# Two mixture-of-experts FFNs around an attention: idle turns on TensorE, ScalarE's relu ahead of its square, row statistics joined and a rounding cut in four on GpSimd

## The chip, the core and the metric

The kernel runs on one core of one Trainium2 chip. The metric is the device time of one execution in microseconds (us), as the median of several runs. The core has five engines that run side by side, each in its own order, and meet at semaphores: TensorE (PE, matrix products), VectorE (DVE), ScalarE (ACT), GpSimd (POOL) and SyncE (SP, which here only starts transfers). TensorE reads its operands from SBUF and writes into eight banks of PSUM. GpSimd works in SBUF only.

## The reference, cut to what matters

4096 tokens of width 128 pass three layers, each behind a layer norm without weights and each added to its input:

```python
x = x + 0.5 * ffn(_layernorm(x), ...)
x = x + attention(_layernorm(x), ...)       # 4096 memory keys and values, one head, plus bias bo
x = x + 0.5 * ffn(_layernorm(x), ...)       # the same weights again

# ffn: 8 experts, the best 2 of each token, hidden width 176, and a shared expert of the same width
scores = sigmoid(x @ gate_w.T);  _, sel = top_k(scores + expert_bias, 2)
h      = square(relu((x * score) @ w_up[e].T in bf16));  routed = h @ w_down[e].T
shared = square(relu(x @ shared_w_up.T)) @ shared_w_down.T      # fp32
out    = sum over the 2 experts + shared
```

## The kernel before

**Tiling.** The tokens lie as 32 tiles of 128 and are worked on in 8 groups of 512. In an FFN all eight experts are computed for each group: the hidden units of the experts fill 11 chunks of 128 rows, taken as six slots k = 0 to 5 (five pairs and a single chunk). For each slot TensorE makes `up(G, k)` (line 1130), VectorE takes relu times the routing weight (`relu_weighted`, line 904, line 901 for the single chunk), ScalarE squares (`square`, line 566), and TensorE adds `down(G, k)` (line 1139). The shared expert goes beside it in fp32: `shared_up_product` (1095), `shared_relu` on ScalarE (555), `shared_square` (560), `shared_down` (1146). `copy_yT` (576) takes the group's sum out of PSUM, `transpose_back` (1112) turns it, and `residual` (912) adds it to X.

**Ahead of the group.** Groups are prepared three ahead (`AHEAD`): row statistics on VectorE (`bn_stats`, 778, then four `bn_aggr`, 786, with a memset between), mean and inverse deviation on GpSimd (`inverse_deviation`, 389 to 392), `normalize` on GpSimd (399), transposes on TensorE (1072), `copy_xT` on ScalarE (543), a cast on GpSimd (`cast_xT`, 423), the gate product (1087), and the routing on VectorE (`route_group`, 16 small steps, lines 853 to 891) for two groups at a time: steps 0 to 8 in a group with even number, steps 9 to 15 in the next. `spread_weights` (GpSimd, 413), `transpose_weights` (1104) and `copy_wbc` (571) bring the weights to the hidden rows.

**Beside it.** In the first FFN GpSimd also splits the attention's keys and values into two fp32r parts, one block of 1024 columns in each group: `kv_hi` (a cast, 454) and `kv_lo` (a subtraction, 456). In the attention it makes `p_lo` (464).

**Order.** Everything is written out by hand: each engine runs its instructions in the order of the code, and a wait holds up all that stands behind it on that engine. G counts the groups of both FFNs (0 to 15), i those of one FFN, n the layer norms (0 to 7 first FFN, 8 to 15 attention, 16 to 23 second FFN). Names are buffers that several things share: `probsT` also holds the hidden rows, `E` the routing weights and the staged keys, `probs` and `xq` the transposed input, `banks` is all of PSUM.

## Time and profile before

| | us |
|---|---|
| median of 3 runs (lowest, highest) | 672.46 (672.07, 672.78) |
| the profiled execution, its own time | 673.28 |
| its span in the trace | 671.6 |
| busy in it: TensorE, VectorE, ScalarE, GpSimd | 614.0, 535.2, 461.3, 381.2 |

The first FFN takes the span up to about 119 us, the attention goes on to about 581 us, the second FFN to the end. Busy times are sums over stages with different limits, so the shares don't tell what a change in one stage is worth. For that the chain of waits is read: it follows the last instruction back, at each step to what released it. The timeline of one engine then shows what stands beside such a step. Where a line says `x2`, two instructions are merged.

### The profile page before, as it was taken

What the parts mean: (1) busy time and instruction counts of PE and PEld (TensorE: products, weight loads), DVE (VectorE), ACT (ScalarE), POOL (GpSimd) and SP (SyncE); (2) the same over time, 40 slices, a digit from 0 to 9 for tenths busy, and PEclk for the clock granted to TensorE, in tenths of its full rate; (3) what the DMA queues carried; (4) which work ended last, traced back from release to release, by engine and by line L of the source; (5) the groups of instructions that cost most, each with busy time, mean ns of one, the idle gap of its engine ahead of it and who ended that gap; (6) DMA issues with size and microseconds to landing.
All of it is one profiled execution on the core that took longest, in us unless ns stands there. A gap on an engine that the chain in (4) does not pass through costs nothing.

```text
span 671.6 us, 9169 instructions
## 1 busy us (share of the span) xinstructions
PE 614.0 (91%) x2784; PEld 431.5 (64%) x2800; DVE 535.2 (80%) x968; ACT 461.3 (69%) x765; POOL 381.2 (57%) x378
## 2 busy tenths in 40 slices
PE   3888989769889999999999999999999997999997
PEld 2445434547667877777777778787777866645542
DVE  4799877748888888887797897887898764799885
ACT  3576778436668767777677786776776863577886
POOL 3856660025367766767687587586687874533100
PEclk9899999869999999999999999999999996999999
DMA  8011110042563553743734626527446330000000
GB/s 296 2 53 42 61 34 0 4 122 62 127 151 86 142 129 77 167 103 89 167 91 120 154 65 158 122 69 176 103 97 153 86 77 1 0 18 16 32 33 31
DMA packets 35555, 59.06 MB, mean 88 GB/s; under 512 B 8539, under 2 KB 9139, under 8 KB 35379
## 3 DMA queue, kind: packets, MB, share of 16 engines
q1 hardware_dynamic: 31891, 53.75, 31.8%
q10 hardware_dynamic: 3616, 4.73, 2.7%
q8 instruction: 23, 0.38, 0.3%
q14 instruction: 25, 0.20, 0.1%
HBM read 8.12 MB, written 2.10 MB: 15 GB/s over the span
## 4 chain that ended last, share of the span: by engine, by line
PE 64%; DVE 19%; issue 6%; ACT 4%; POOL 2%; SPq 2%; ACTq 1%; DMA 1%; DVEq 0%; POOLq 0%
PE banks L1254 7%; PE banks L1256 7%; PE banks L1255 7%; PE banks L1295 7%; PE banks L1297 6%; PE banks L1296 6%; PE banks L1274 4%; DVE bank_max L1007 4%; PE banks L1130 4%; DVE E L1002 3%; PE banks L1139 3%; DVE probsT L904 3%; PE banks L1146 3%; PE banks L1305 2%; PE banks L1095 2%
## 5 line engine op out<-in xcount | busy, mean ns | idle before, releaser
L464 POOL TENSOR_TENSOR p_lo<-probsT,p_hi 128x768 fp32r<-128x768 f32 (+1 forms) x128 | 226.4, 1773 | 173.5 <-ACT p_hi L659 173.2
L1007 DVE TENSOR_REDUCE bank_max<-banks 128x1 f32<-128x1024 f32 x128 | 156.1, 1219 | 34.3 <-PE banks L1256 33.5
L659 ACT ACTIVATE p_hi<-probsT 128x768 fp32r<-128x768 f32 (+1 forms) x128 | 104.5, 816 | 23.0 <-PE banks L1297 19.1
L1254 PE MATMUL banks<-kv_lo,q_parts 128*128 128x512 f32 x256 | 112.9, 441 | 5.1 <-ACT E L677 3.6
L566 ACT ACTIVATE probsT<-probsT 128x1024 bf16<-128x1024 bf16 x96 | 92.2, 980 | 34.5 <-DVE probsT L904 31.3
L1002 DVE STREAM_TRANSPOSE E<-E 128x1024 f32<-128x1024 f32 x92 | 113.5, 1234 | 0.4 <-ACT E L677 0.2
L904 DVE SCALAR_TENSOR_TENSOR probsT<-banks,E 128x1024 bf16<-128x1024 f32 x80 | 95.5, 1218 | 22.0 <-PE banks L1130 20.2
L1295 PE MATMUL banks<-p_hi,kv_lo 128*128 128x512 f32 x256 | 108.7, 424 | 0.4 <-ACT attended L696 0.3
L651 ACT ACTIVATE p_hi<-banks 128x256 fp32r<-128x256 f32 (+1 forms) x128 | 52.3, 408 | 81.2 <-PE banks L1274 81.0
L677 ACT ACTIVATE E<-banks,neg_max 128x1024 f32<-128x1024 f32 x92 | 102.3, 1112 | 6.7 <-DVE neg_max L1013 4.8
L1296 PE MATMUL banks<-p_lo,kv_hi 128*128 128x512 f32 x256 | 102.9, 402 | 0.0
L1297 PE MATMUL banks<-p_hi,kv_hi 128*128 128x512 f32 x256 | 102.7, 401 | 0.0
L1256 PE MATMUL banks<-kv_hi,q_parts 128*128 128x512 f32 x256 | 102.6, 401 | 0.0
L1255 PE MATMUL banks<-kv_hi,q_parts 128*128 128x512 f32 x256 | 102.4, 400 | 0.0
L995 DVE TENSOR_TENSOR p_lo<-banks,p_hi 128x256 fp32r<-128x256 f32 (+1 forms) x128 | 56.1, 438 | 45.5 <-ACT p_hi L651 45.1
L1274 PE MATMUL banks<-ident,probs 128*128 128x128 f32 x272 | 53.9, 282 | 10.9 <-ACT probs L687 6.7
L1274 PEld LDWEIGHTS banks<-ident,probs 128*128 128x128 f32 x272 | 37.2, 144 | 33.7 <-DVE p_lo L995 7.4
L1254 PEld LDWEIGHTS banks<-kv_lo,q_parts 128*128 128x128 f32 x256 | 49.2, 192 | 14.0 <-ACT E L677 4.7
L1295 PEld LDWEIGHTS banks<-p_hi,kv_lo 128*128 128x128 f32 x256 | 48.7, 190 | 13.6 <-issue 2.7
L1130 PE MATMUL banks<-E,wup_b 128*128 128x512 bf16 x166 | 50.3, 384 | 7.0 <-ACT probsT L555 6.1
L1297 PEld LDWEIGHTS banks<-p_hi,kv_hi 128*128 128x128 f32 x256 | 48.6, 190 | 12.4
L1256 PEld LDWEIGHTS banks<-kv_hi,q_parts 128*128 128x128 f32 x256 | 48.8, 191 | 11.6
(110 smaller groups left out, 887.5 us busy)
## 6 DMA issues: line engine op xcount, KB each, us to landing
probsT<-E SPq DMA_DIRECT2D x248, 128.0 KB, 2.4
probsT<-E SPq DMA_DIRECT2D x168, 64.0 KB, 2.0
E<-in_keys_values SPq DMA_DIRECT2D x8, 512.0 KB, 3.5
probsT<-E ACTq DMA_DIRECT2D x56, 64.0 KB, 2.4
out<-X SPq DMA_DIRECT2D x8, 256.0 KB, 2.1
X<-in_x SPq DMA_DIRECT2D x1, 1280.0 KB, 9.1
probsT<-E ACTq DMA_DIRECT2D x8, 128.0 KB, 4.1
X<-in_x SPq DMA_DIRECT2D x3, 256.0 KB, 5.3
```

The source lines that it names most:

```text
L464: pool.tensor_tensor(moved_part(p_lo, ring), moved_pair(ring // UP, ring % UP), moved_part(p_hi, ring).bitcast(fp32), ALU.subtract).then_i ...
L659: act.activation(moved_part(p_hi, ring), moved_pair(ring // UP, ring % UP), ACT.Copy).then_inc(moved_hi_done, 1)
L904: dve.scalar_tensor_tensor(hidden[:, k, :, :], up_banks[PAIR_BANK[k]], 0.0, spread.unsqueeze(1).to_broadcast([P, 2, N]), ALU.max, ALU.mult ...
L1002: dve.transpose(half, half).then_inc(squares_done, 1)
L1007: dve.tensor_reduce(bank_max[:, i % 2, h:h + 1], score_pair(u, i, h).rearrange("p b n -> p (b n)"), AX.X, ALU.max).then_inc(bank_max_done, 1)
L1254: pe.matmul(bank, qh, kl, start=True, stop=False)
L1255: pe.matmul(bank, ql, kh, start=False, stop=False)
L1256: pe.matmul(bank, qh, kh, start=False, stop=True).then_inc(scores_done, 1)
L1274: last = pe.transpose(TB[:, at_column:at_column + P], own_exponentials(w, t)[:, c * P:(c + 1) * P], ident[:, :])
L1295: pe.matmul(OB, vl, hi, start=(c == 0), stop=False)
L1296: pe.matmul(OB, vh, lo, start=False, stop=False)
L1297: pe.matmul(OB, vh, hi, start=False, stop=(c == KC - 1)).then_inc(pv_done, 1)
```

## The change

Five things, all around the FFNs:

- GpSimd takes over, for the layer norms n = 4 to 8, what `bn_aggr` did: `join_halves` makes mean and variance of a row from the two halves that `bn_stats` leaves. Eight small instructions stand where three were, and VectorE's memset and four `bn_aggr` go. VectorE's next `bn_stats` waits for GpSimd's reads instead.
- The subtraction that makes `kv_lo` is cut into four quarters of 256 columns, issued one behind the other without a wait between them.
- On ScalarE `square(G, 0)` goes behind `shared_relu(G)` and `copy_yT(G - 1)`, in all groups but the very first.
- TensorE turns the identity 24 times before its first real work: 12 when the constants are set, 8 when the first statistics are there, 4 when the first inverse deviation is there.
- The first group of X is loaded in two halves, by SP's and by ScalarE's queue.

```diff
+def joins_on_pool(n):
+    return AHEAD < n <= ATTENTION_LN
...
-            sp.dma_start(X[:, 0:GT, :], x[:, 0:GT, :]).then_inc(x_loaded[0], 16)
+            sp.dma_start(X[:, 0:GT // 2, :], x[:, 0:GT // 2, :]).then_inc(x_loaded[0], 16)
...
+            def join_halves(n):
+
+                step = POOL_STEPS * (n - AHEAD - 1)
+                means = stats[:, :, :].rearrange("p t (a b) -> p t a b", b=3)[:, :, :, 1]
+                sums = stats[:, :, :].rearrange("p t (a b) -> p t a b", b=3)[:, :, :, 2]
+                pool.tensor_scalar(half_means[:, :, :], means, -0.5, None, ALU.mult).then_inc(joined, 1)
+                pool.tensor_tensor(squares_sum[:, :], sums[:, :, 0], sums[:, :, 1], ALU.add).then_inc(joined, 1)
+                pool.wait_ge(joined, step + 1)
+                pool.tensor_tensor(half_gap[:, :], half_means[:, :, 0], half_means[:, :, 1], ALU.subtract
+                                   ).then_inc(joined, 1)
+                pool.tensor_tensor(neg_mean[:, :], half_means[:, :, 0], half_means[:, :, 1], ALU.add
+                                   ).then_inc(moments_read, 1)
+                pool.wait_ge(joined, step + 3)
+                pool.tensor_tensor(gap_squared[:, :], half_gap[:, :], half_gap[:, :], ALU.mult).then_inc(joined, 1)
+                pool.tensor_scalar(squares_sum[:, :], squares_sum[:, :], 1.0 / D, EPS, ALU.mult, ALU.add
+                                   ).then_inc(joined, 1)
+                pool.wait_ge(joined, step + 5)
+                pool.tensor_tensor(var_eps[:, :], gap_squared[:, :], squares_sum[:, :], ALU.add
+                                   ).then_inc(moments_read, 1)
+                pool.wait_ge(moments_read, 2 * n + 2)
+                pool.tensor_tensor(rstd[:, :], var_eps[:, :], minus_half[:, :], ALU.pow).then_inc(rstd_done, 1)
...
-                        pool.tensor_tensor(kv_lo[:, i, :], kv_stage[:, i % 2, :], kv_hi[:, i, :].bitcast(fp32),
-                                           ALU.subtract).then_inc(kv_lo_done, 1)
+                        for a in range(0, KVW, KVW // 4):
+                            part = slice(a, a + KVW // 4)
+                            last = pool.tensor_tensor(kv_lo[:, i, part], kv_stage[:, i % 2, part],
+                                                      kv_hi[:, i, part].bitcast(fp32), ALU.subtract)
+                        last.then_inc(kv_lo_done, 1)
...
+            act.dma_start(X[:, GT // 2:GT, :], x[:, GT // 2:GT, :]).then_inc(x_loaded[0], 16)
...
-                    square(G, 0)
                     if f or i:
                         shared_relu(G)
+                    if i:
+                        copy_yT(G - 1)
+                    square(G, 0)
                     if f and i == 0:
                         copy_y(LAST)
-                    if i:
-                        copy_yT(G - 1)
...
             def aggregate(n):
+                if joins_on_pool(n):
+                    return
...
+            def warm_up():
+
+                pe.wait_ge(consts_set, 1)
+                turn_identity(12)
+                pe.wait_ge(stats_done, 1)
+                turn_identity(8)
+                pe.wait_ge(rstd_done, 1)
+                turn_identity(4)
```

ScalarE, around the start of group 2 in the first FFN, before. Line 566 is `square`, 555 the shared relu, 576 `copy_yT`, 543 `copy_xT`:

```order
24 L566 ACTIVATE probsT<-probsT 128x512
25 L566 ACTIVATE probsT<-probsT 128x1024
26 L555 ACTIVATE probsT<-banks 88x1024
27 L576 ACTIVATE probsT<-banks 128x512
28 L543 ACTIVATE xq<-banks 128x512
29 L566 ACTIVATE probsT<-probsT 128x1024
```

The same place after, where `square` is line 615, the relu 604, `copy_yT` 625 and `copy_xT` 592:

```order
25 L615 ACTIVATE probsT<-probsT 128x512
26 L604 ACTIVATE probsT<-banks 88x1024
27 L625 ACTIVATE probsT<-banks 128x512
28 L615 ACTIVATE probsT<-probsT 128x1024
29 L592 ACTIVATE xq<-banks 128x512
30 L615 ACTIVATE probsT<-probsT 128x1024
```

The square of the group's slot 0 has moved behind the relu and `copy_yT`; it now stands directly ahead of `copy_xT`.

GpSimd, from one group to the next in the first FFN, before. Line 454 is `kv_hi`, 456 `kv_lo`, 389 to 392 the inverse deviation, 413 the spread weights, 423 the cast of the next input:

```order
38 L454 CAST kv_hi<-E 128x1024
39 L456 TENSOR_TENSOR kv_lo<-E,kv_hi 128x1024
40 L389 TENSOR_TENSOR neg_mean<-moments,minus_one 128x4
41 L390 TENSOR_TENSOR var_eps<-moments,eps 128x4
42 L392 TENSOR_TENSOR rstd<-var_eps,minus_half 128x4
43 L413 COPY probsT<-weight 128x1024
44 L423 CAST E<-xq 128x512
```

The same place after:

```order
43 L499 CAST kv_hi<-E 128x1024
44 L503 TENSOR_TENSOR kv_lo<-E,kv_hi 128x256 x4
45 L408 TENSOR_SCALAR half_means<-stats 128x8
46 L409 TENSOR_TENSOR squares_sum<-stats 128x4
47 L411 TENSOR_TENSOR half_gap<-half_means 128x4
48 L413 TENSOR_TENSOR neg_mean<-half_means 128x4
49 L416 TENSOR_TENSOR gap_squared<-half_gap 128x4
50 L417 TENSOR_SCALAR squares_sum<-squares_sum 128x4
51 L420 TENSOR_TENSOR var_eps<-gap_squared,squares_sum 128x4
52 L423 TENSOR_TENSOR rstd<-var_eps,minus_half 128x4
53 L458 COPY probsT<-weight 128x1024
54 L468 CAST E<-xq 128x512
```

One subtraction has become four, and the three instructions ahead of the spread weights have become eight.

## Rows read from the trace of the kernel before

**Rows 1.** The page's first part: busy us, share of the span, instructions.

```profile
PE 614.0 (91%) x2784; PEld 431.5 (64%) x2800; DVE 535.2 (80%) x968; ACT 461.3 (69%) x765; POOL 381.2 (57%) x378
```

**Rows 2.** Chain of waits, groups 2 to 4 of FFN one: start, duration, what.

```profile
55.78 1.86 DVE route L877
...
62.91 1.01 ACT probsT L555
...
66.78 0.44 PE banks L1104 x4
...
76.01 0.79 PE banks L1087 x8
76.80 0.46 PE banks L1130 x2
```

**Rows 3.** Timeline of VectorE, group 4: start, duration, line, operation.

```profile
78.43 0.35 DVE L872 TENSOR_SCALAR route<-expz 128x64 f32<-128x64 f32 x1
...
79.40 1.85 DVE L877 TENSOR_TENSOR route<-route,ebias 128x64 f32<-128x64 f32 x1
```

**Rows 4.** Timeline of GpSimd in the same stretch.

```profile
77.69 1.04 POOL L454 CAST kv_hi<-E 128x1024 fp32r<-128x1024 f32 x1
78.81 2.36 POOL L456 TENSOR_TENSOR kv_lo<-E,kv_hi 128x1024 fp32r<-128x1024 f32 x1
```

**Rows 5.** Line 877, whole span: duration ns lowest/median/highest, first and last start.

```profile
L877 DVE TENSOR_TENSOR route<-route,ebias x9: 192/224/1855, 13.3 to 634.3; 128x64 f32<-128x64 f32 x7, 128x32 f32<-128x32 f32 x2
```

**Rows 6.** Timeline of VectorE in FFN two, where GpSimd is idle.

```profile
633.46 0.18 DVE L872 TENSOR_SCALAR route<-expz 128x64 f32<-128x64 f32 x1
```

**Rows 7.** Timeline of both engines at 575 us: VectorE waits beside two GpSimd instructions.

```profile
575.62 1.28 POOL L464 TENSOR_TENSOR p_lo<-probsT,p_hi 128x512 fp32r<-128x512 f32 x1 [0.80 <-ACT p_hi L659]
576.88 1.91 POOL L399 TENSOR_SCALAR xn<-X,neg_mean,rstd 128x128 f32<-128x128 f32 x4
...
575.88 1.30 DVE L817 CAST E<-probs 128x512 bf16<-128x512 f32 x1
```

**Rows 8.** Timeline of ScalarE, start of group 3, then of group 4.

```profile
61.95 1.06 ACT L566 ACTIVATE probsT<-probsT 128x1024 bf16<-128x1024 bf16 x1 [0.50 <-DVE probsT L904]
...
72.34 1.06 ACT L566 ACTIVATE probsT<-probsT 128x1024 bf16<-128x1024 bf16 x1 [0.48 <-DVE probsT L904]
73.31 1.00 ACT L555 ACTIVATE probsT<-banks 88x1024 f32<-88x1024 f32 x1
...
74.75 0.60 ACT L543 ACTIVATE probs<-banks 128x512 f32<-128x512 f32 x1
```

**Rows 9.** Timeline of GpSimd, group 4, then the spread weights of group 3.

```profile
73.74 0.20 POOL L390 TENSOR_TENSOR var_eps<-moments,eps 128x4 f32<-128x4 f32 x1
74.02 1.01 POOL L392 TENSOR_TENSOR rstd<-var_eps,minus_half 128x4 f32<-128x4 f32 x1
...
64.83 1.04 POOL L413 COPY probsT<-weight 128x1024 f32<-128x1024 f32 x1 [0.20 <-DVE weight L891]
```

**Rows 10.** Timeline of VectorE, statistics of group 4.

```profile
72.23 0.86 DVE L778 BATCH_NORM_STATS2 stats<-X 128x6 f32<-128x128 f32 x4
...
73.23 0.28 DVE L786 BATCH_NORM_AGGREGATE moments<-stats 128x2 f32<-128x6 f32 x3
```

**Rows 11.** Chain of waits, group 5 of the second FFN.

```profile
639.77 1.01 ACT probsT L555
```

**Rows 12.** Timeline of TensorE, first group, then a later shared up product.

```profile
8.43 1.09 PE L1072 MATMUL banks<-ident,xn 128*128 128x128 f32 x4 [8.43 <-DVE xn L797]
...
18.52 3.62 PE L1095 MATMUL banks<-xq,sup_s 128*88 128x512 f32 x4
...
47.70 1.88 PE L1095 MATMUL banks<-probs,sup_s 128*88 128x512 f32 x4
```

**Rows 13.** Chain of waits, first microseconds.

```profile
0.72 3.49 DMA X<-in_x
```

**Rows 14.** TensorE by stretch: length, busy us (instructions), granted clock, transfers' share, GB/s.

```profile
25.00:26.00 1.00, 0.24 (x2) 0.77 0.00 0
```

More of the change, by code:

```diff
@@ L59, with moments_before @@
 Q_HALF = 5
+def joins_on_pool(n):
+    return AHEAD < n <= ATTENTION_LN
+POOL_STEPS = 5
+def moments_before(n):
+    return sum(not joins_on_pool(k) for k in range(n))
 ATTENTION_LN = GROUPS
@@ L772, in statistics @@
             def statistics(n, g):
-                wait(dve, moments_done, n)
+                if joins_on_pool(n - 1):
+                    dve.wait_ge(moments_read, 2 * n)
+                else:
+                    wait(dve, moments_done, moments_before(n))
                 if n >= SECOND_LN:
@@ L781, in aggregate @@
             def aggregate(n):
+                if joins_on_pool(n):
+                    return
                 dve.wait_ge(stats_done, n + 1)
@@ L1141, in down, with turn_identity @@
                 last.then_inc(down_done, 1)
+            def warm_up():
[5 more added lines that the diff above has]
+                turn_identity(4)
+            def turn_identity(times):
+                for _ in range(times):
+                    pe.transpose(up_banks[0][:, 0, 0:P], ident[:, :], ident[:, :])
             def shared_down(G):
```

14 lines of the change are left out of this document (11 added, 3 removed).

## The prediction, made before the changed kernel ran

> **What bounds the kernel now.** I read the page's busy times first, to see that no engine is full: TensorE is busy 614.0 of 671.6 us, the others less [rows 1]. So waits decide, and they differ by stage. The change touches only the FFNs, so I then followed the chain of waits through two neighbouring groups of the first FFN [rows 2]. It has two kinds of stretch. From 66.78 us to 76.80 us every link is TensorE: the odd group is bound by its products. Ahead of that, from the relu of slot 3 in group 2, the chain leaves TensorE: routing steps and relus on VectorE, then the shared relu on ScalarE (62.91 us), then TensorE again. The longest link there is line 877, 1.86 us for an addition on 128x64 values. The same instruction has a median of 0.22 us over its nine times [rows 5]. In group 4 it ends at 81.25 us, just behind GpSimd's `kv_lo`, which ends at 81.17 us [rows 3, 4]: it waits for the SBUF port that GpSimd holds. This happens in groups 0, 2 and 4, where `kv_lo` stands beside it, with 1.6 us of waiting in each: some 4.8 us of the span.
>
> **The quarters.** A GpSimd subtraction takes 1.28 us at 512 columns [rows 7] and 2.36 us at 1024 [rows 4], so 2.1 ns a column and 0.2 us besides; at 256 columns I estimate 0.7 us, and 2.8 us for the four, 0.45 us more for each block. GpSimd is busy for 57% of the span [rows 1] and, with the block done, stands idle until the next statistics, so that is hidden. Line 877 starts 0.6 us behind `kv_lo` and would find the port free after 0.1 us, if the waiting engine gets it between two instructions. Rows 7 say it does: a cast of VectorE waits for one GpSimd instruction, ends at 577.18 us, and the next four on GpSimd take 1.91 us instead of 1.76. But line 877 isn't the only step with two SBUF inputs. Line 855 behind it now meets the second quarter (about 0.4 us), and lines 858 and 862 behind slot 4's relu the third and fourth (0.1 to 0.3 us). So of 1.6 us I count 1.0 us at slot 4's relu and 0.9 us at the next group's slot 0.
>
> The Trainium skill (page "SBUF — State Buffer", section "Who interferes with whom") says that the shared port pair is an exclusive lock held for a whole instruction, and that a VectorE instruction with two SBUF inputs contends with a GpSimd instruction that reads SBUF; lines 877 and 456 bear that out, 81.25 us against 81.17 us.
>
> **ScalarE's order.** At the start of an odd group the shared relu stands behind `square` of slot 0, and that waits 0.50 us for VectorE's slot 0 [rows 8]. With the relu first it can start behind the square of slot 5, at 61.45 us instead of 62.91 us, and `copy_yT` and `copy_xT` follow 0.5 us earlier than now. TensorE's next products then wait no more for the relu but for slot 0 and slot 1 from VectorE, so VectorE's time is what counts. At the start of an even group it goes the other way: there the relu waits for the shared product and starts at 73.31 us either way, and the square, which today runs in ScalarE's idle time at 72.34 us, is put between `copy_yT` and `copy_xT` [rows 8]. `copy_xT` (74.75 us) and with it the cast on GpSimd come 0.9 us later, `down` of slot 0 waits for the square until 75.8 us, and the gate product, now at 76.01 us, starts at about 76.3 us. **Cost 0.3 us** at the relu of slot 3, which opens the VectorE stretch.
>
> GpSimd's 0.9 us has a second effect: `kv_hi` moves to about where line 872 starts. Line 872 runs 0.35 us beside it today, 0.18 us where GpSimd is idle [rows 3, 6]. At worst it waits for all of `kv_hi` (0.9 us), at best it goes ahead of it. Walking through both orders, slot 4's relu comes 0.56 us or 0.96 us earlier than now, slot 0's 0.45 or 0.65 us. I take 0.55 us, all of the above included.
>
> **The join.** VectorE loses the memset and four `bn_aggr`. `bn_stats` ends at 73.09 us and the last `bn_aggr` at 73.51 us [rows 10]; since neighbours on VectorE overlap by some 0.07 us, that is 0.35 us, in groups 0 to 4. On GpSimd's way from the statistics to the inverse deviation a dependent instruction starts 0.28 us behind its source (73.74 us to 74.02 us) [rows 9]. Five such steps, counting those whose wait an independent one fills in part, and the power at 1.01 us make 2.4 us, against 1.94 us now (73.09 us to 75.03 us). So the inverse deviation comes 0.5 us later, measured from `bn_stats`. In even groups the cast behind it waits for `copy_xT` anyway. In odd groups the spread weights stand behind it; they start 0.20 us behind its end today [rows 9] and would be 0.34 us late. They are done at 65.87 us now and TensorE transposes them at 66.78 us [rows 2], so 0.8 us of that is spare, and a group that comes forward by d at slot 0 comes forward by d + 0.45 us at the weights' transposes, where VectorE's 0.35 us is already in. The new wait, `bn_stats` on GpSimd's reads, has a whole group of time.
>
> **By pair of groups.** Groups 2 and 3: 0.55 + 0.45 = **1.0 us**. Groups 4 and 5: group 5 has no statistics, so **0.6 us**. Groups 0 and 1: no change of ScalarE's order in group 0, but the join is there 1.0 us longer in GpSimd's order and shifts `kv_hi` onto line 872; slot 0 gains 0.3 to 0.9 us, the pair **0.9 us**. Groups 6 and 7 have neither routing nor gate; relu first and square first come out within 0.1 us, since slot 1's relu and square decide. First FFN: **2.5 us less**.
>
> **The second FFN** has only the new order on ScalarE. Group 0 there pays 0.45 us (`copy_y` and `copy_xT` stand behind the square), given back but for 0.3 us in group 1; the next pair costs 0.1 us, and groups 4 and 5 gain 0.2 us, since the relu is on the chain there [rows 11]. **0.2 us more.**
>
> **The start.** The first transposes take 1.09 us for four, and the shared product takes 3.62 us there and 1.88 us later [rows 12]. That is the lower clock of 1.2 GHz (the record of the granted clock starts later, so the durations tell it). The 24 turns at 0.27 us each (1.09 us / 4) fill 1.9 to 8.4 us, so the first real transposes at 8.43 us start neither later nor, I think, on the critical path if faster: GpSimd's second normalization doesn't wait for them, and the gaps up to 18.5 us stay. The shared product at 18.52 us is what the next group waits for, and I take it to be slow still. Its worth is 0 to 0.1 us. The load of X takes 3.49 us [rows 13]; half the bytes on each of two queues, with the next load close behind, I put at 0.1 us less (0.3 less to 0.2 more). **0.1 us less.**
>
> **Sum:** 0.9 + 1.0 + 0.6 - 0.2 + 0.1 = 2.4 us less. From the profiled execution, 673.28 us, that gives 670.9 us; the median of the runs before stands 0.8 us under it, so the predicted median is 672.46 - 2.4 = **670.1 us**.
>
> **Rivals.**
> 1. *The clock stays up.* If the turns keep TensorE at 2.4 GHz until 22 us, the shared product ends 1.7 us sooner, and the next group's input with it: 670.1 - 1.8 = 668.3 us. Against it: between the first transposes and 13 us TensorE has only the gate product. After it first rose, it fell back within the stretch from 25 to 26 us, whose mean is 0.77 of full speed, with TensorE busy for 0.24 us [rows 14]. Chance 0.1.
>
> The Trainium skill (page "TensorE: Matmul & The Clock Gate", Part 1) says that the throttled state is the default and activity releases it, which is what the turns would use; by that rule the time would be this rival's only if the activity afterwards holds it.
>
> 2. *More comes through.* Line 872 goes ahead of `kv_hi`, the later steps miss the quarters, and relu first shortens the odd groups by more than VectorE's share: 0.7 us more in each of three pairs, 668.0 us. Chance 0.15.
> 3. *Eaten.* `kv_hi` takes line 872's time in full, the join makes the weights late, and TensorE, the bound of odd groups, gives nothing back: 671.1 to 673 us, 672.0 us as the middle. Chance 0.2.
> 4. *Slower: the four quarters hold the port together.* They are issued without a wait between them. If VectorE doesn't get in, line 877 waits until the end of the fourth: `kv_lo` ends 0.45 us later than now and starts up to 0.9 us later, so each of three groups loses up to 1.3 us instead of gaining 0.55, and with 0.3 us of the new order the total is 3 x 0.9 us more: 675 us. It decides as soon as VectorE misses two boundaries. Rows 7 speak against it, though GpSimd's instructions there are of two kinds. Chance 0.1.
>
> **Numbers.** My forecast (669.1 to 671.1 us, 0.45) and the rivals above. A measurement of this kernel tells about 0.2% (1.3 us) from no change. Faster by more than that: 0.45 + 0.1 + 0.15 = 0.70; within: 0.20; slower: 0.10. The range leaves out the slower rival and the tail of the first two together: 667.4 to 672.9 us.
>
> **What would show it.** Line 877 in groups 0, 2 and 4 at 0.3 us or less, with line 872 up to 1.1 us in one or two of them; `kv_lo` in four of 0.7 us; `copy_xT` of even groups behind the square; the chain of odd groups without the shared relu; the shared product at 18.5 us still at 3.6 us (if at 1.9, rival 1). Line 877 at 2 us or more in spite of the quarters is rival 4. Wrong I would be if the attention's length changed by more than 1 us, since nothing in it is touched.

## The result and the profile after

| | median us | lowest to highest | runs |
| --- | --- | --- | --- |
| before | 672.36 | 670.02 to 673.72 | 15 |
| changed | 674.08 | 671.56 to 677.78 | 15 |

The ratio is 1.0038, with an interval of 1.0023 to 1.0053: the changed kernel is **slower by 0.4%**, where I had forecast 2.4 us less. The ratio is estimated from the runs together with its interval and isn't the quotient of the medians: these lie 1.7 us apart, and the ratio stands for 2.6 us. Below, what a part is worth in us is its ratio less one, times the median before. The profiled execution of the changed kernel took 676.66 us, near the upper end of its runs, with a span of 675.0 us. A second one (e8, below) took 674.34 us.

The page's first part for the changed kernel, which answers to [rows 1]:

```profile
PE 623.6 (92%) x2808; PEld 435.8 (65%) x2824; DVE 530.2 (79%) x943; ACT 460.4 (68%) x765; POOL 390.2 (58%) x427
```

VectorE has 25 instructions less, GpSimd 49 more and TensorE the 24 turns. TensorE is busy for 9.6 us more, although the turns take 6.0 us of it (two rows of 2.82 and 3.15 us). The other 3.6 us fit the stretches at the lower clock below; I haven't added them up.

The part of the change that I had worked out in most detail came out. The timeline of VectorE in group 4 of the first FFN (start, duration, line, operation), which answers to [rows 3]; lines 926, 931 and 909 are lines 872, 877 and 855 of before:

```profile
76.26 0.72 DVE L926 TENSOR_SCALAR route<-expz 128x64 f32<-128x64 f32 x1
...
77.59 0.22 DVE L931 TENSOR_TENSOR route<-route,ebias 128x64 f32<-128x64 f32 x1
...
78.11 0.39 DVE L909 TENSOR_TENSOR route<-route,best 128x64 f32<-128x64 f32 x1
```

The addition of 1.85 us takes 0.22 us. Line 926 takes 0.72 us instead of 0.35 us. GpSimd in the same stretch shows why, beside [rows 4] and [rows 9]: the first instruction of the join, its last (the power), and then `kv_hi` across the start of line 926, with `kv_lo` in four of 0.70 us behind it.

```profile
70.54 0.25 POOL L408 TENSOR_SCALAR half_means<-stats 128x8 f32<-128x8 f32 x1 [0.37 <-DVE stats L830]
...
72.06 1.04 POOL L423 TENSOR_TENSOR rstd<-var_eps,minus_half 128x4 f32<-128x4 f32 x1
...
75.88 1.04 POOL L499 CAST kv_hi<-E 128x1024 fp32r<-128x1024 f32 x1
77.01 2.78 POOL L503 TENSOR_TENSOR kv_lo<-E,kv_hi 128x256 fp32r<-128x256 f32 x4
```

The chain of waits through the same groups (start, duration, what) has no long piece of line 931 left, but two pieces that [rows 2] doesn't have: ScalarE's `copy_yT` and `square` ahead of TensorE at the start of group 4, and a gap of 2.37 us in group 5, behind which four transposes take 1.09 us, as at the lower clock in [rows 12].

```profile
71.51 0.58 ACT probsT L625
72.09 0.95 ACT probsT L615
...
73.09 0.61 PE banks L1193 x2
...
86.40 2.37 issue
88.77 1.09 PE banks L1158 x4
```

### The profile page after: what moved, and what is told of

The parts are those of the page before. It is cut to its first block, busy times and chain, and to the rows that moved or that the text cites. A ratio compares the mean times of both kernels' runs of the same rounds, so it can differ in the third digit from the quotient of the medians.

```text
span 675.0 us, 9236 instructions
## 1 busy us (share of the span) xinstructions
PE 623.6 (92%) x2808; PEld 435.8 (65%) x2824; DVE 530.2 (79%) x943; ACT 460.4 (68%) x765; POOL 390.2 (58%) x427
## 4 chain that ended last, share of the span: by engine, by line
PE 56%; DVE 18%; issue 6%; SPq 6%; ACT 5%; POOL 4%; DMA 3%; ACTq 1%; DVEq 0%; POOLq 0%
PE banks L1321 6%; SPq L330 6%; PE banks L1323 6%; PE banks L1322 6%; PE banks L1362 5%; PE banks L1363 5%; PE banks L1364 5%; DVE probsT L958 4%; PE banks L1341 4%; PE banks L1193 3%; DVE bank_max L1061 3%; PE banks L1184 3%; DVE E L1056 3%; PE banks L1213 3%; PE banks L1149 2%
## 5 line engine op out<-in xcount | busy, mean ns | idle before, releaser
L1363 PEld LDWEIGHTS banks<-p_lo,kv_hi 128*128 128x128 f32 x256 | 48.8, 191 | 11.7 <-issue 1.7
```

The lines of the kernel that those rows point to most:

```text
L1363: pe.matmul(OB, vh, lo, start=False, stop=False)
```

## How the traces are compared

All the kernels below have the same instructions on TensorE around the shared down product, which opens once in each group. So the distance from one start of that product to the next is a ruler. Its start in groups 1 and 2 of the kernel before, and of the kernel of e2:

```profile
44.69 1.88 PE L1146 MATMUL banks<-probsT,sdown_s 88*128 88x512 f32 x4
...
54.99 0.60 PE L1146 MATMUL banks<-probsT,sdown_s 88*128 88x512 f32 x1
```

```profile
46.02 1.88 PE L1146 MATMUL banks<-probsT,sdown_s 88*128 88x512 f32 x4
...
56.80 0.59 PE L1146 MATMUL banks<-probsT,sdown_s 88*128 88x512 f32 x1
```

54.99 - 44.69 = 10.30 us before, and 10.78 us in e2. From such rows comes this table, us, with the last column the distance between groups 0 and 7 of the second FFN (1 to 2 is from group 1 to group 2 of the first):

| kernel | ratio (interval) | 1 to 2 | 2 to 3 | 3 to 4 | 4 to 5 | 5 to 6 | 2nd FFN |
| --- | --- | --- | --- | --- | --- | --- | --- |
| before | | 10.30 | 13.31 | 10.31 | 14.87 | 9.47 | 74.49 |
| before again (e16) | | 10.30 | 13.32 | 10.30 | 14.89 | 9.47 | 74.49 |
| e1 quarters | 0.9952 (0.9934 to 0.9970) | 10.30 | 11.97 | 10.30 | 13.52 | 9.47 | 74.49 |
| e2 ScalarE's order | 1.0055 (1.0032 to 1.0078) | 10.78 | 13.64 | 10.78 | 15.19 | 9.83 | 75.43 |
| e3 join | 0.9993 (0.9971 to 1.0014) | 10.31 | 13.43 | 10.31 | 15.15 | 9.48 | 74.19 |
| e4 start | 1.0015 (0.9994 to 1.0037) | 10.30 | 13.31 | 10.30 | 14.87 | 9.48 | 74.48 |
| e5 all but the order | 0.9968 (0.9952 to 0.9984) | 10.30 | 12.10 | 10.30 | 13.82 | 9.47 | 74.20 |
| e6 quarters, join | 0.9945 (0.9926 to 0.9964) | 10.31 | 12.09 | 10.31 | 13.81 | 9.47 | 74.21 |
| e7 quarters, order in odd groups | 0.9961 (0.9936 to 0.9985) | 10.30 | 11.99 | 10.30 | 14.12 | 10.58 | 74.51 |
| e8 the change again | 1.0022 (1.0000 to 1.0044) | 10.77 | 12.06 | 10.77 | 14.74 | 10.67 | 75.14 |
| the change | 1.0038 (1.0023 to 1.0053) | 10.78 | 12.05 | 10.78 | 15.35 | 9.87 | 75.13 |
| e11 quarters, copies first | 0.9977 (0.9954 to 0.9999) | 11.25 | 12.29 | 11.24 | 13.86 | 9.82 | 74.49 |
| e12 e6, order in groups 1, 3 | 0.9961 (0.9939 to 0.9982) | 10.30 | 11.99 | 10.30 | 13.83 | 9.47 | 74.20 |
| e13 order in group 5 | 1.0011 (0.9995 to 1.0027) | 10.30 | 13.31 | 10.31 | 15.55 | 10.47 | 74.49 |
| e14 order in the second FFN | 1.0008 (0.9990 to 1.0027) | 10.31 | 13.31 | 10.30 | 14.87 | 9.47 | 75.43 |

Where the code of a stretch is the same and the clock stays up, the distances agree within 0.02 us, so a shift of 0.1 us in this table is a real one. The times of whole runs spread over 2.6 to 8.8 us for one kernel.

The last column opens at the shared down product of group 0 and leaves out what the order does inside that group. From the shared up product to the shared down product of group 0 in the second FFN, in the kernel before and in e14:

```profile
581.31 1.88 PE L1095 MATMUL banks<-xq,sup_s 128*88 128x512 f32 x4
...
588.64 1.88 PE L1146 MATMUL banks<-probsT,sdown_s 88*128 88x512 f32 x4
```

```profile
579.29 1.88 PE L1101 MATMUL banks<-xq,sup_s 128*88 128x512 f32 x4
...
587.07 1.88 PE L1152 MATMUL banks<-probsT,sdown_s 88*128 88x512 f32 x4
```

That is 7.33 us against 7.78 us. The other thirteen profiles with the square first there have 7.31 to 7.33 us, the other three with the relu first there (the change, e2, e8) 7.77 or 7.78 us: 0.45 us more, on top of the last column.

## The parts alone: e1 to e4

**e1**, `kv_lo` in quarters:

```
-    pool.tensor_tensor(kv_lo[:, i, :], kv_stage[:, i % 2, :], ...
+    for a in range(0, KVW, KVW // 4):
+        ...
```

> The kernel before with kv_lo in four quarters alone. The prediction's step: VectorE's addition of 128x64 values behind slot 3's relu falls from 1.86 us to 0.3 us or less in groups 0, 2 and 4, kv_lo takes 4 x 0.7 us; 0.5 to 1.0 us in each of three pairs of groups comes forward, so about 2 us less in the first FFN. Theory A (the attention's loss is the clock's, set off by an earlier start): the first FFN is 2 us shorter and the attention 1 to 3 us longer, ratio 0.998 to 1.002. Theory B (the attention's loss comes from the turns of the identity or the split load): nothing is lost behind, ratio 0.997.

668.23 us against 671.51 us, ratio 0.9952: 3.2 us less. In groups 2 and 4 the stretch is shorter by 1.34 and 1.35 us, where I had counted 1.0 us. The groups 0 and 1 can be read only roughly, since the clock differs at the start: the shared down product of group 1 starts at 42.45 us in e11, which has e1's code up to there, but at 44.89 us in e1 itself, and at 44.00 to 44.69 us in five profiles without the quarters (before, e10, e13, e14, e16). VectorE in group 4 (line 880 is line 877 of before, line 858 line 855):

```profile
77.28 0.35 DVE L875 TENSOR_SCALAR route<-expz 128x64 f32<-128x64 f32 x1
...
78.25 0.23 DVE L880 TENSOR_TENSOR route<-route,ebias 128x64 f32<-128x64 f32 x1
...
78.77 0.39 DVE L858 TENSOR_TENSOR route<-route,best 128x64 f32<-128x64 f32 x1
```

The addition gains 1.62 us, and the two later steps give 0.17 and 0.10 us back. Nothing eats the gain behind the FFN: theory B holds here, and the prediction's rival 4 falls.

**e2**, the shared relu ahead of the square of slot 0, in all groups:

```
-                    square(G, 0)
                     if f or i:
                         shared_relu(G)
+                    if i:
+                        copy_yT(G - 1)
+                    square(G, 0)
```

> The kernel before with ScalarE's shared relu ahead of the square of slot 0 alone. The prediction: about 0 in the first FFN (odd groups gain up to 0.5 us, even groups lose 0.3 us and push kv_hi onto VectorE), 0.2 us more in the second. The pair of profiles says 0.65 us more in the second FFN. If that is this order's: ratio 1.001, the attention's length as before. If the second FFN's loss was the clock's, its length here is within 0.2 us of the kernel before.

674.73 us, ratio 1.0055: 3.7 us **more** (interval 2.1 to 5.2), the largest effect of all parts. The traces place 3.4 us of it: 2.0 us in the first FFN between groups 1 and 7, and in the second 0.45 us in group 0 and 0.94 us behind it. ScalarE at the start of group 4, which answers to [rows 8]; then TensorE (`down` of slot 0) and VectorE's line 872:

```profile
75.38 1.02 ACT L555 ACTIVATE probsT<-banks 88x1024 f32<-88x1024 f32 x1 [1.38 <-PE banks L1095]
...
76.77 1.05 ACT L566 ACTIVATE probsT<-probsT 128x1024 bf16<-128x1024 bf16 x1
77.72 0.59 ACT L543 ACTIVATE probs<-banks 128x512 f32<-128x512 f32 x1
...
78.11 0.38 PE L1139 MATMUL banks<-probsT,wdown_b 128*128 128x512 bf16 x1 [0.38 <-ACT probsT L566]
...
81.05 0.69 DVE L872 TENSOR_SCALAR route<-expz 128x64 f32<-128x64 f32 x1
```

The relu starts when the shared product ends, in either order. Before, the square had been done in the time that ScalarE waited for it ([rows 8], 72.34 us). Now it comes behind, and TensorE waits for it. Laid on the kernel before by the relu's start, `down` of slot 0 is 0.4 us later; laid by the preceding shared down product the whole group is 0.48 us later. `copy_xT` is 0.83 us later, and with it the cast, the normalization and `kv_hi` on GpSimd, which so meets line 872: 0.69 us instead of 0.35 us. Each even group costs 0.48 + 0.34 = 0.82 us. The chain then runs over VectorE, so all that follows is late by as much.

**e3**, the join on GpSimd:

```
-                pool.wait_ge(moments_done, n + 1)
+                if joins_on_pool(n):
+                    ...
+                    join_halves(n)
+                    return
```

> The kernel before with the rows' statistics of groups 3 to 8 joined on GpSimd alone. The prediction: 0.35 us less on VectorE in each of groups 0 to 4, the inverse deviation 0.5 us later; 0.2 to 0.4 us a pair, about 0.8 us less in the first FFN, ratio 0.999. If the join makes the spread weights late, the first FFN is as long as before or longer by up to 0.5 us. Nothing behind the first FFN changes by theory B; by theory A the attention takes part or all of the gain back.

672.09 us beside 671.51 us, but ratio 0.9993: no difference that can be measured. The table says what it does: 0.12 us more from group 2 to 3, 0.28 us more from 4 to 5, and 0.30 us less from group 0 to 1 of the second FFN, where the join isn't. GpSimd's way from the statistics is the cause of the first two: in the changed kernel it takes 72.06 + 1.04 - 70.54 = 2.56 us from the start of its first instruction to the end of the power. In group 4 of the kernel before, the cast behind the power stood idle for 0.39 us for ScalarE's copy:

```profile
75.42 0.61 POOL L423 CAST E<-probs 128x512 bf16<-128x512 f32 x1 [0.39 <-ACT probs L543]
```

In e6 it starts right behind the power and waits for nothing, so the later power pushes it and `kv_hi` behind it, which comes 0.31 us later than in the same group of e1 (9.69 us and 9.38 us behind the shared down product of group 3). VectorE in group 4 of e6, which has both edits:

```profile
75.73 0.64 DVE L925 TENSOR_SCALAR route<-expz 128x64 f32<-128x64 f32 x1
```

That is 0.29 us more than in e1 (0.35 us). The gain of the second FFN I can't explain: VectorE's row for slot 5's relu there shows a wait of 0.20 us put down to no other engine in e1 and none in e6, in the same code. It isn't chance: the step from group 0 to 1 there is 12.57 or 12.58 us in all six profiles with the join and 12.86 or 12.87 us in the twelve without.

**e4**, the start: the turns and the load in halves:

```
-            sp.dma_start(X[:, 0:GT, :], x[:, 0:GT, :]).then_inc(x_loaded[0], 16)
+            sp.dma_start(X[:, 0:GT // 2, :], x[:, 0:GT // 2, :]).then_inc(x_loaded[0], 16)
...
+            act.dma_start(X[:, GT // 2:GT, :], x[:, GT // 2:GT, :]).then_inc(x_loaded[0], 16)
...
-                    pe.wait_ge(consts_set, 1)
+                    warm_up()
```

> The kernel before with the start's edits alone: TensorE's 24 turns of the identity, and the load of X in two halves on two queues. Theory B (the attention's loss comes from here, from the split load's queues or the turns): the attention is 2 to 4 us longer and the ratio is 1.003 to 1.006. Theory A: the load lands about 0.4 us later, the first FFN is 0 to 0.4 us longer, the rest as before, ratio 1.000 to 1.001.

672.16 us, ratio 1.0015 with 1 inside its interval, and the attention takes 475.9 us beside 476.2 us before: it is not the start's edits that lengthen it. Theory B, which I held for that part, is wrong. The sum of the four parts is -0.48% - 0.07% + 0.55% + 0.15% = +0.15%, and 1.0038 and 1.0022 were measured for the whole.

## Together: e5, e6 and e8

**e5** is the changed kernel without the order:

```
+                    square(G, 0)
                     if f or i:
                         shared_relu(G)
-                    if i:
-                        copy_yT(G - 1)
-                    square(G, 0)
```

> The changed kernel with ScalarE's old order (square of slot 0 ahead of the shared relu), all else of the change kept. If the order is what makes the changed kernel slower, as the part alone says (ratio 1.0055, 3.7 us): 1.0038 - 0.0055 = 0.998, so 670 us beside a kernel before of 671.5 us, and the first FFN is some 2 us shorter and the second some 0.6 to 1.0 us shorter than in the changed kernel. If the parts disturb each other in the attention instead: the ratio stays above 1.001 and the attention is 2 us or more longer than before.

669.38 us, ratio 0.9968. With the order it is 672.97 us on the same chip (e8): the order costs 3.6 us inside the change as alone. **It is what made the change slower**: without it the change would have been faster by 0.3%. The table says where, e8 less e5: 0.47 us in each of the steps 1 to 2 and 3 to 4 and nothing from 2 to 3 (there the join has already brought `kv_hi` onto line 872, so the order has nothing to add), 0.92 us from 4 to 5, 1.20 us from 5 to 6, and 0.94 us in the second FFN, 4.0 us, and with the 0.45 us of the second FFN's group 0 it is 4.4 us in all.

**e6** keeps only `kv_lo` in quarters and the join (diffs of e1 and e3).

> The kernel before with the two edits that gained alone: kv_lo in quarters and the join on GpSimd. Sum of the parts: 0.9952 and 0.9993, so 0.9945 (667.8 us). If the join stands in the quarters' way on GpSimd, or TensorE bounds what is left, 0.9955 or more.

667.79 us, ratio 0.9945, as the sum of its parts: faster than both kernels, and the lowest ratio of all. e1 alone is within its interval, so what the join adds to it isn't shown.

**e8** is the changed kernel again, with no edit.

> The changed kernel once more, for a second profile. If the 4 us that its first profile loses in the attention between 200 and 210 us belong to the change, they are there again. If it is the clock's chance in one execution, the attention is within 1.5 us of the kernel before, the time is again 1.002 to 1.005, and the loss stands in the two FFNs.

Ratio 1.0022, attention 476.1 us beside 480.3 us in the first profile. The 4 us that the first profile loses between 200 and 210 us aren't the change's. There ScalarE's exponentials wait for SP's moves of strips, and TensorE idles behind them. The first profile of the change, ScalarE; then TensorE by stretch in it, and in the kernel before again (e16): length, busy us (instructions) of PE, PEld, DVE, ACT, POOL, granted clock, transfers' share, GB/s.

```profile
202.46 1.11 ACT L726 ACTIVATE E<-banks,neg_max 128x1024 f32<-128x1024 f32 x1 [3.25 <-DMA probsT<-E]
```

```profile
200.00:205.00 5.00, 2.71 (x13) 1.94 (x12) 2.36 (x3) 2.54 (x5) 1.37 (x2) 0.95 0.65 137
205.00:210.00 5.00, 5.00 (x18) 3.94 (x17) 3.21 (x5) 2.91 (x7) 4.39 (x3) 0.71 0.28 66
```

```profile
200.00:205.00 5.00, 4.05 (x11) 3.22 (x12) 2.74 (x3) 3.73 (x7) 3.03 (x2) 0.66 0.38 94
```

The kernel before has the same wait (2.80 us) and a fall of the clock in its second profile, e16, and neither in its first; the changed kernel's second profile (e8) has a wait of 2.23 us. Over the eighteen profiles of this study the attention, whose code is the same but for the first rows' statistics, takes 471.1 to 480.3 us from the last shared down product of the first FFN to the first of the second.

## Which groups, and which step: e7, e11, e12, e13, e14

**e7**, quarters, and the relu first in the odd groups of the first FFN only:

```
+                    relu_first = f == 0 and i % 2 == 1
+                    if not relu_first:
+                        square(G, 0)
...
+                    if relu_first:
+                        square(G, 0)
```

> kv_lo in quarters and the relu first in the odd groups of the first FFN only (groups 1, 3, 5, 7); the even groups and the second FFN keep the square first. The prediction's step: odd groups gain up to 0.5 us each, so 0.5 to 1.0 us less than quarters alone, ratio 0.9945. The trace of the order alone says that the odd groups lose 0.3 us each, since slot 1's square comes 0.2 us later and stands on the chain: 0.6 us more than quarters alone, ratio 0.996.

Both expectations miss. Groups 1 and 3 are as long as in e1 within 0.02 us: the odd group neither gains nor loses. In e2, laid over the kernel before at the shared down product of group 1, the relu of group 3 starts 0.74 us earlier, while VectorE's steps are 0.82 us late ahead of the relu and 0.82 us late behind it. The clearer view is e7 beside e1. ScalarE's relu and VectorE's slot 1 in group 3, first e1, then e7:

```profile
61.77 1.00 ACT L558 ACTIVATE probsT<-banks 88x1024 f32<-88x1024 f32 x1
...
63.54 1.22 DVE L907 SCALAR_TENSOR_TENSOR probsT<-banks,E 128x1024 bf16<-128x1024 f32 x1
```

```profile
57.78 1.00 ACT L558 ACTIVATE probsT<-banks 88x1024 f32<-88x1024 f32 x1
...
61.11 1.22 DVE L911 SCALAR_TENSOR_TENSOR probsT<-banks,E 128x1024 bf16<-128x1024 f32 x1
```

Measured from the shared down product of group 1 (44.89 us and 42.44 us), the relu comes at 15.34 us instead of 16.88 us, 1.54 us earlier, and VectorE's step at 18.67 us instead of 18.65 us. The relu and VectorE had been equally late; taking one away leaves the other. Group 5 costs 0.60 + 1.11 = 1.7 us, by another mechanism (e13).

**e11**, quarters, and in the even groups of the first FFN the order relu, `copy_yT`, `copy_xT`, square:

```
+                    even = f == 0 and i and i % 2 == 0
+                    if not even:
+                        square(G, 0)
...
                         copy_xT(n + AHEAD, G + AHEAD, i + AHEAD, xT_bank)
...
+                    if even:
+                        square(G, 0)
```

> kv_lo in quarters, and in the even groups of the first FFN the order relu, copy_yT, copy_xT, square of slot 0: the copy that GpSimd's cast waits for goes ahead of the square, which in the change it stands behind. Two causes are told apart. Group 1 to 2 (shared down to shared down): 10.30 us with the square first, 10.78 us in the change; if the late square on TensorE's path is the cause, it is 10.9 us or more here; if the late copy_xT is, 10.3 us. Group 2 to 3: 11.97 us with quarters alone, and 0.35 us more in the change, put down to kv_hi that comes onto VectorE's line 872 because copy_xT is late; with copy_xT early that part is gone and line 872 takes 0.35 us or less, not 0.70 us. Ratio 0.996 to 0.998, against 0.9952 of quarters alone.

The first cause is decided: 11.25 us, 0.95 us more, so it is the late square that TensorE waits for. The second expectation misses: `kv_hi` is on time and line 872's counterpart takes 0.22 us, yet group 2 to 3 is 0.32 us longer than in e1. TensorE and VectorE in group 2 (line 879 is line 872 of before, line 884 line 877):

```profile
50.73 0.38 PE L1146 MATMUL banks<-probsT,wdown_b 128*128 128x512 bf16 x1 [0.99 <-ACT probsT L569]
```

```profile
53.52 0.22 DVE L879 TENSOR_SCALAR route<-expz 128x64 f32<-128x64 f32 x1
...
54.36 0.78 DVE L884 TENSOR_TENSOR route<-route,ebias 128x64 f32<-128x64 f32 x1
```

VectorE's steps are later against GpSimd, which isn't, so the addition now falls on a quarter of `kv_lo` (0.78 us instead of 0.23 us). A shift of one engine doesn't remove the meeting, it moves it to another step.

**e12**, e6 with the relu first in groups 1 and 3 (the diff of e7 with `i in (1, 3)`):

> kv_lo in quarters, the join, and the relu first in groups 1 and 3 alone. With both off its path (statistics' tail and relu) the odd group can come forward, where each alone gave nothing: 0.4 us less in group 3 and as much in group 1 than quarters and join (0.9945), and no late q_high in group 5: 0.9935. If the two together give nothing either: 0.9945, and group 2 to 3 is 12.09 us as there.

668.57 us, ratio 0.9961: not better than e6. Group 2 to 3 is 11.99 us, 0.10 us less than in e6 where 0.4 us had been expected. A third wait takes over, the spread weights from GpSimd, late by the join. In group 3 of e12 they end at 63.58 us, and TensorE, idle for 0.31 us, starts to transpose them:

```profile
62.54 1.04 POOL L458 COPY probsT<-weight 128x1024 f32<-128x1024 f32 x1
```

```profile
63.67 0.63 PE L1161 MATMUL banks<-ident,probsT 128*128 128x128 f32 x4 [0.31 <-issue]
```

**e13**, the kernel before with the relu first in group 5 alone (the diff of e7 with `i == 5`):

> The kernel before with the relu first in group 5 of the first FFN alone. There ScalarE's q_high stands behind slot 1's square; with the relu first TensorE reaches its wait for q_low 0.9 us earlier, so it idles 2.37 us instead of 1.49 us (as in e2, e7, e8), and the end of the wait stays. If that longer idle stretch lets the clock fall in a part of the runs (it did in e7, e8 and the changed kernel, not in e2; 1.1 to 1.7 us each): ratio 1.0010 to 1.0020. If the clock there is chance either way: 1.0000.

Ratio 1.0011, interval 0.9995 to 1.0027: in the middle between the two expectations, and open by the times. The trace shows the mechanism. TensorE in group 5, the project product, the gap, and what follows:

```profile
87.34 1.10 PE L1241 MATMUL banks<-xq,wq_scaled 128*128 128x512 f32 x2
88.28 0.59 PE L1136 MATMUL banks<-E,wup_b 128*128 128x512 bf16 x2
91.24 0.63 PE L1110 MATMUL banks<-ident,probsT 128*128 128x128 f32 x4 [2.37 <-issue]
...
92.19 1.49 PE L1136 MATMUL banks<-E,wup_b 128*128 128x512 bf16 x3
93.47 2.88 PE L1152 MATMUL banks<-probsT,sdown_s 88*128 88x512 f32 x4
```

The same place in the kernel before:

```profile
91.93 0.63 PE L1104 MATMUL banks<-ident,probsT 128*128 128x128 f32 x4 [1.49 <-issue]
```

TensorE comes earlier to a wait whose end stays, and idles for 2.37 us, where it was 1.49 us. The code says what it waits for: VectorE's `q_low`, which follows ScalarE's `q_high`. That starts 11.68 us behind the shared down product of group 4 in both kernels, since slot 1's square ahead of it waits for VectorE. Then the clock falls: three products take 1.49 us (0.81 us in the kernel before), and the shared down product 2.88 us (1.88 us). It costs 0.68 + 1.00 = 1.7 us. It fell behind this gap in four of the five profiles that have it (the change, e7, e8, e13, not e2), and in none of the thirteen with the gap of 1.5 us.

**e14**, the relu first in the second FFN alone (the diff of e7 with `f == 1`):

> The kernel before with the relu first in all groups of the second FFN alone. The profiles of e2 and e8 put 0.94 us there (0.48 us in groups 2, 4 and 6, less 0.36 us, plus 0.36 us): ratio 1.0014. The prediction had 0.2 us: 1.0003.

The distance from group 0 to 7 is 75.43 us, 0.94 us more, as in e2, and group 0 has 0.45 us more ahead of it. The whole time, ratio 1.0008, can't tell that from 0.

## The start: e9, e10, e15, e16

**e9**, the turns alone:

```
-                    pe.wait_ge(consts_set, 1)
+                    warm_up()
```

> The kernel before with the 24 turns of the identity alone (the load of X whole). The start's two edits together came to 1.0015 (0.9994 to 1.0037), and what e5 has over e6 is 0.0023. If the turns cost it: 1.001 or more, and the attention between its units 3 and 4 takes 52 us or more as in all four profiles with the start's edits. If they cost nothing: 0.999 to 1.001. In the first FFN the shared product of group 0 ends at the same time as before within the spread of the profiles so far (2.5 us).

673.07 us, ratio 1.0026 (1.0009 to 1.0044): the turns **cost** 0.6 to 3.0 us. The steps of the table are as before, so the place is ahead of group 1. TensorE's clock there, by stretch:

```profile
24.00:26.00 2.00, 1.21 (x9) 0.59 (x8) 1.72 (x9) 1.14 (x2) 1.93 (x5) 0.70 0.00 0
26.00:28.00 2.00, 2.00 (x7) 1.26 (x8) 1.57 (x5) 0.87 (x2) 1.85 (x4) 0.50 0.00 0
```

It falls at about 25 us and stays at half over the rest of group 0. The turns had not raised it early here. The first transposes take 1.12 us and the first gate product 1.84 us:

```profile
10.47 1.84 PE L1087 MATMUL banks<-gate_s,xq 128*128 128x8 f32 x8 [0.78 <-ACT xq L543]
```

That is as long as without turns (1.09 and 1.85 us), and e4 has 1.12 and 1.85 us. In e5, e8 and e15 the first transposes take 0.66 us and the gate product 1.03 us, so there the clock rose before them, and in the change between the two. In the other profiles with turns it is either this (e4) or the whole shared product at half (3.62 us: e5, e8, e15), and in one neither (the change, 2.49 us). So five of six starts with turns are slow in one of the two ways. Without turns it is three of twelve (before, e1, e2).

**e10**, the load in halves alone (the first two diffs of e4):

> The load of X for group 0 in two halves on two queues alone. The statistics start at 4.65 us instead of 4.23 us, as in the changed kernel, so up to 0.4 us more: ratio 1.000 to 1.001. If the split is what lengthens the attention's units 3 and 4 by 1.6 us: 1.002 and 52 us or more there.

672.77 us, ratio 1.0007 (0.9986 to 1.0029), no difference that can be measured. The changed kernel's chain, beside [rows 13]:

```profile
0.73 3.90 DMA X<-in_x
```

3.90 us in halves on two queues, 3.49 us whole on one. But the load varies from profile to profile: whole it takes 3.16 to 3.91 us in thirteen (3.49 us in the middle), in halves 3.48 to 3.90 us in five (3.70 us in the middle). The halves gain nothing; that they lose something isn't shown.

**e15**, nine turns more, in the gaps:

```
                         transpose_for_ffn(g, g)
+                        turn_identity(3 if g == 0 else 2)
...
                         gate(g, g)
+                        if g == 0:
+                            turn_identity(4)
```

> The turns of e9 and nine more: 3 behind the first transposes, 4 behind the first gate product, 2 behind the second transposes, so that TensorE has hardly a gap from 1.9 us on. If the clock then stays up, the shared product of group 0 takes 1.9 us instead of 2.5 to 3.6 us, the gate products 1.0 us instead of 1.85 us, and the first shared down product starts at 28 to 29.5 us instead of 29.6 to 34.5 us: ratio 0.997 (the prediction's rival 1). If the clock falls anyway after the start, the turns delay the real work by up to 0.5 us: ratio 1.002 to 1.003 as e9.

Ratio 1.0018 (1.0003 to 1.0033), near the second expectation. The clock comes up early and doesn't stay. TensorE, two of the groups of transposes, and its clock by stretch:

```profile
8.14 0.66 PE L1072 MATMUL banks<-ident,xn 128*128 128x128 f32 x4 [0.49 <-DVE xn L797]
...
13.21 1.12 PE L1072 MATMUL banks<-ident,xn 128*128 128x128 f32 x4 [2.11 <-POOL xn L399]
```

```profile
8.00:10.00 2.00, 1.41 (x11) 1.20 (x12) 1.24 (x10) 1.17 (x2) 0.56 (x3) 1.00 1.08 414
...
12.00:14.00 2.00, 0.80 (x4) 0.80 (x5) 1.69 (x10) 0.00 (x0) 1.15 (x3) 0.50 0.93 384
...
20.00:22.00 2.00, 2.00 (x4) 0.69 (x3) 1.92 (x12) 0.00 (x0) 1.37 (x4) 0.50 0.00 0
```

The first transposes take 0.66 us instead of 1.09 us [rows 12], but they are waited for by nobody. The clock falls in the gap of 2.11 us, in which TensorE waits for GpSimd's normalization, and is at half until 22 us, over the whole of the shared product (3.62 us), which is waited for.

**e16**, the kernel before again.

> The kernel before once more, for a second profile of it. If the stage lengths that differ between kernels with the same code in a stage (29.6 to 34.5 us to the first shared down product, 471 to 480 us for the attention) are the clock's chance, this profile differs from the first of the kernel before by 1 to 3 us in one of them, and by less than 0.05 us in the steps from group 1 to group 4 of the first FFN.

Its steps agree with the first profile within 0.02 us. The first shared down product starts at 30.02 us (31.61 us), and the attention takes 474.6 us (476.2 us). Its shared product of group 0 takes 2.60 us, 1.0 us less than the 3.62 us of [rows 12], in the same kernel. Among the kernels that have before's code up to group 1 but for the start's edits, that group's shared down product starts at 44.69, 44.45, 44.00, 44.02 and 44.20 us without turns (before, e10, e13, e14, e16), and at 45.30, 45.35 and 44.64 us with them (e4, e9, e15): about 1 us later in the middle. That bears the times out in sign and roughly in size, on three profiles. Why the turns make the slow starts more frequent isn't shown, and an early rise isn't the reason in e4 and e9, which had none.

## Why the prediction was wrong

**The quarters** were right in mechanism and too small: 1.35 us a pair and 3.2 us in all, where I had 1.0 us for slot 4's relu and cut it to 0.55 us for `kv_hi`'s shift. Lines 855 and 858 give back 0.27 us together, where I had 0.4 us for the first alone. VectorE does get in between two instructions of GpSimd. With this and the other parts, line 877's counterpart takes 0.22 to 0.27 us in the changed kernel.

**ScalarE's order is the step that failed**: I had it near nothing in the first FFN and at 0.2 us in the second, and it costs 3.6 to 3.7 us. It went wrong in four places. *Even groups:* I had priced the square at 0.3 us; it costs 0.48 us on TensorE's path, and alone another 0.34 us through GpSimd, where `kv_hi` meets line 872 (I had named that meeting, and counted it in the 0.55 us). Group 6, where I had 0.1 us at most, costs 0.36 us (e2). *Odd groups:* I had credited them with up to 0.5 us for the relu's earlier start, though I had written that VectorE's time then counts; VectorE was as late as the relu, and the gain is 0.00 us. *Group 5*, which I hadn't looked at: `q_high` on the reordered engine keeps its time, TensorE's gap ahead of it grows by 0.88 us, and the clock falls behind it, up to 1.7 us. *Second FFN:* I had 0.2 us. Group 0 costs the 0.45 us that I had, but no part of it is given back in group 1 (12.87 us in e2, 12.86 us before), where I had all but 0.3 us. Groups 2 and 3 cost 0.47 us, where I had 0.1 us. The gain in group 5 came (0.36 us), but group 4 costs 0.47 us, where I had 0.2 us of gain for both, and group 6 another 0.36 us: 0.45 + 0.94 = 1.39 us.

By pairs of groups of the first FFN, us:

| groups | forecast | the change | e8 | e5, without the order |
| --- | --- | --- | --- | --- |
| 1 to 3 | -1.0 | -0.78 | -0.78 | -1.21 |
| 3 to 5 | -0.6 | +0.95 | +0.33 | -1.06 |
| 5 to 7 | 0 | +0.40 | +1.20 | +0.01 |

Each is two steps of the table less the same steps before. For groups 0 and 1, where I had 0.9 us less, there is no such step: group 1's shared down product starts at 42.82 us in the change and 44.49 us in e8, against 44.69 and 44.20 us before, and the clock of the start decides. The forecast for 1 to 3 was near by luck: the quarters gave more than I had (-1.34 us in e1) and the order took more (+0.43 us between e5 and e8). The later pairs and the second FFN broke the sum. The shifts that need no fall of the clock come to 3.4 us in e2, where the times say 3.7 us. How often the clock falls in group 5 over many runs stays open (e13).

**The join** was near on GpSimd's way and wrong on who waits. From the end of `bn_stats` to the end of the power it takes 2.66 us in the changed kernel (70.44 to 73.10 us) against 1.94 us before: 0.7 us later, where I had 0.5 us. I had written that in even groups the cast waits for `copy_xT` anyway. It did, but for 0.39 us only, and the rest of the 0.7 us pushes `kv_hi` onto line 872 (0.3 us). VectorE's 0.35 us in odd groups ran into the relu, in the old order, and into the spread weights, in the new one (e12), as rival 3 had it. I had added 0.45 us for relu and join together at the weights' transposes of group 3; of that 0.10 us came (e12 beside e6).

**The start** was 0.1 us less in the sum and cost some 1 us (e4, with 0 inside its interval; the turns alone, e9, are clear of it). The load in halves is 0.2 us later in the middle of the profiles, at the edge of what I had set, and its spread is wider than that. The turns start the first transposes no later, as forecast, but I had bounded them by 0 from below. What they cost is in how the clock falls afterwards, and I hadn't asked for that.

**The attention**: I had written that its length within 1 us would show that nothing was touched. It varies by 9 us between profiles with the same code, so that was no test. Of the rivals, rival 3 (eaten) is nearest in mechanism, and its time was too short. The slower one that I had named blamed the quarters; it should have been the reordered engine.

In sum: predicted -2.4 us. By the parts, measured alone: quarters -3.2, join -0.5 (0 within its interval), order +3.7, start +1.0 (0 within its interval); together +1.0 us, where the two measurements of the whole gave +1.5 and +2.6 us.

## What to carry to other kernels

Before an instruction is moved ahead of another on an in-order engine, look at what fills that engine's waiting time in each variant of the group. Work that ran for nothing in a gap costs time behind it (0.48 us a group of the square's 1.06 us here), and every engine fed from that queue gets the delay, so count the meetings it makes there. Where two paths arrive within 0.1 us of one another, removing one gives nothing, and a third may be waiting behind them: price the pair, not the one. Shortening work ahead of a wait whose end stays fixed makes TensorE idle longer, and that can drop its clock for the products behind.

## What the runs showed of the hardware

- A long GpSimd instruction cut in four costs it 0.42 us (2.78 us instead of 2.36 us), and a VectorE instruction that waits beside it loses 0.00 to 0.55 us (e1, e11) in place of 1.63 us. That agrees with what the prediction took from the Trainium skill (page "SBUF — State Buffer", section "Who interferes with whom") about a lock held for a whole instruction.
- TensorE kept its clock over the gap of 1.5 us in group 5 in thirteen profiles, and lost it behind the gap of 2.4 us in four of five. No run here shows what decides it in the fifth.
- Early turns on TensorE raised its clock before the first transposes in three of six profiles (0.66 us for four in e5, e8, e15), just behind them in one (the change), and not in two (1.12 us in e4 and e9). Where it rose, it was back at half by 12 to 14 us, with the work that mattered still to come. Whoever heats up for one product has to look where the next gap is.
- One load took 3.16 to 3.91 us whole on one queue (thirteen profiles) and 3.48 to 3.90 us in halves on two (five): halves gained nothing.
- Runs of one kernel spread by 2.6 to 8.8 us here (0.4 to 1.3%). The profiles of kernels with the same code in a stretch differ mainly in the clock, in two places: the first group (29.7 to 34.5 us to its shared down product in the five profiles that have before's code up to there: before, e2, e13, e14, e16) and the attention (471 to 480 us). The distance between two landmarks in the trace resolves 0.02 us, so the parts of a change can be read there when the times can't tell them.
